# Graph attention layer: the running sum is carried through TensorE's accumulation, and ScalarE instead of VectorE writes it back and rescales it

## The chip, the core and the metric

One core of one Trainium2 chip (trn2) runs the whole program in one launch. The metric is the device time of one execution in microseconds (us). The kernel before takes 2374.6 us, the median of three executions (2372.0 to 2375.01).

## The reference

A two-layer graph network on 3125 nodes of 256 features and 53125 edges, sorted by destination. Layer 0 makes edge messages with a small MLP and an attention over heads, and sums them per node. Layer 1, in which the change lies, is a graph attention layer with four heads of 64:

```python
h = (x @ W).reshape(n, NHEAD, OUT_FEATS)
h_l = (a_l * h).sum(-1)
h_r = (a_r * h).sum(-1)
e = h_l[row] + h_r[col]
e = jnp.where(e > 0, e, ALPHA * e)
m = jax.ops.segment_max(e, row, num_segments=n)
ex = jnp.exp(e - m[row])
denom = jax.ops.segment_sum(ex, row, num_segments=n)
att = ex / (denom[row] + 1e-16)
out = jax.ops.segment_sum(att[:, :, None] * h[col], row, num_segments=n)
```

The kernel makes one pass over the edges: it keeps a running maximum, sums exp(e - running maximum) times h and the plain exponentials side by side, rescales the sum when the maximum moves, and divides at the end.

## The kernel before

Edges are sorted into 232 groups of 256 (two chunks of 128 edges), and every group belongs to one tile of 128 nodes, known only at run time from the table `gt_i`. Four groups are a batch, so there are 58 batches. Each engine runs its own instruction stream in order; the streams are tied by semaphores. In layer 1 every engine has a function `layer1(st)` that `run` calls once per step, unrolled by 16 inside a hardware loop. In step s an engine works on several groups at once, at fixed distances behind s (`st.back(d)` is the group s - d).

What the engines do in layer 1, group by group:

- GpSimd (POOL, `gather1`, L633 to L646) gathers the rows of 256 edges, by two indirect DMAs, into one of 16 slots of `row1_g`. A slot comes free when VectorE has made that slot's messages.
- TensorE (L1556 to L1609), in this order in step s: for an even step the transposition of h_r for a pair of groups (L1565, "hrT"); for group s - 3 the matmuls that spread h_r under a mask into two banks (L1579, L1582, "hr"); once a batch eight small matmuls that spread the maxima (L1594, "hm"); and for group s - 13 the sum of messages per node, two fp32 matmuls with the one-hot matrix `oneh1` as weights, into one of the two banks `agg1` (L1607, "agg").
- ScalarE (ACT, L834 to L890): once a batch index copies (L828, L829), the mask `pen` and the one-hot `onehT1` (L844, L849); once a pair the copy of hrT out of PSUM (L856); for each group two `away` and one `oneh1` activation (L860, L865) and a small copy of h_l (L875, L878, "hl"); once a batch the two exponentials `ew` and `mscale` (L886, L890).
- VectorE (DVE, L1268 to L1328): for each group the running sum of group s - 11 (L1286: tile of `acc1` plus `agg1`), the maximum (L1291), the messages of group s - 8 (L1323, "msg1"); once a batch the rescaling of the tile (L1280), the softmax steps (L1302 to L1315) and the chain of the maximum (L1240 to L1265, `top`).

A tile number is loaded from `gt_i` into registers of the engine that uses it, eight at a time, by `tiles16` (L335 to L340): before, on VectorE for L1286 and on ScalarE for the h_l copies, each twice in 16 steps.

```python
dve.tensor_tensor(acc, acc, agg1[c.slot(2)], ALU.add).then_inc(s("acc1_done"), 1)   # L1286
pe.wait_ge(s("acc1_done"), n - 1)                                                   # L1605
```

Of the kernel before, what the change touches and what calls it, by code (L numbers as in the profile page):

```python
# [30 lines left out]
P = 128  # L31
# [6 lines left out]
AHEAD = 2  # L38


class Step:
# [12 lines left out]
    def real(self):  # L54

        return not isinstance(self.k, int) or 0 <= self.n < self.total

# [32 lines left out]
def gnn_kernel(nc, x, src, dst, edge_attr_64, edge_weight, w1, b1, w2, b2, ln_w, ln_b, wq, bq, wk, bk,  # L90
# [47 lines left out]
    with ExitStack() as ctx:  # L138
# [57 lines left out]
        gt_i = sb("gt_i", [P, 16 + NG + 24], I32)  # L196
        ended = sb("ended", [P, NG])
# [10 lines left out]
        def carve(n):  # L208
# [51 lines left out]
        msg1 = carve(2 * GJ * NH1 * HE).rearrange("p (s c n) -> p s c n", s=2, c=GJ)  # L260
        hrT = carve(2 * 2 * GJ * P // 2).bitcast(BF16).rearrange("p (s n) -> p s n", s=2)
        gt_x, gt_y = (work[:, v:v + NB * ME].rearrange("p (b e) -> p b e", e=ME)
                      for v in (NT * (H + HR), NT * (H + HR) + NB * ME))
        apart = carve(NB * ME * ME).rearrange("p (b e f) -> p b e f", b=NB, e=ME)
        hq_flat = hq.rearrange("p t n -> p (t n)")
        oneh1 = hq_flat[:, 0:16 * GJ * P].rearrange("p (s c n) -> p s c n", s=16, c=GJ)
        rows_bc = work[:, 0:2 * BE].bitcast(BF16).rearrange("p (s n) -> p s n", s=4)
# [11 lines left out]
        away = sb("away", [P, 2, GJ, P])  # L279
        sc = sb("sc", [P, 2, GJ, NH0])  # L280
# [47 lines left out]
        def tiles_of(eng, k, lag, count=8):  # L328

            _, values = nc.values_load_multi_w_load_instructions(  # L330
                gt_i[0:1, bass.ds(k * 8 + (16 - lag), count)], engines=(eng,), min_val=0, max_val=NT - 1,
                skip_runtime_bounds_check_because="the table's values are bounded by the minimum with NT - 1")
            return values

        def tiles16(eng, k, lag, half):  # L335

            _, values = nc.values_load_multi_w_load_instructions(  # L337
                gt_i[0:1, bass.ds(k * 16 + (16 - lag + 8 * half), 8)], engines=(eng,), min_val=0, max_val=NT - 1,
# [22 lines left out]
        def heads_of(rows, st):  # L361

            return rows[:, st.slot(4), :].rearrange("p (h d) -> p h d", d=HE)[:, :, 0:HD1]

# [148 lines left out]
        def _(pool):  # L513
# [138 lines left out]
        def _(act):  # L652
# [167 lines left out]
            act.wait_ge(s("hr_parts"), 2)  # L820
            act_tiles = {}
# [12 lines left out]
            def layer1(st):  # L834
                g, b = st.u % BG, batch(st)
                if g == 0:
# [3 lines left out]
                    if b.real():  # L840
# [16 lines left out]
                if st.real():  # L857
                    act.wait_ge(s("srcC_ready"), b.n + 1)
                    for j in range(GJ):
                        act.activation(away[:, st.slot(2), j, :], iota1[:, :], ACT.Abs,  # L860
                                       bias=srcC[:, b.slot(4), g, j:j + 1], scale=-1.0).then_inc(s("away1"), 1)
                    act.wait_ge(s("away1"), 2 * st.n + 2)
                    if not st.first(16):
                        act.wait_ge(s("agg1_ready"), st.n - 15)
                    act.activation(oneh1[:, st.slot(16), :, :], away[:, st.slot(2), :, :], ACT.Relu, bias=1.0,  # L865
                                   scale=-1.0).then_inc(s("oneh1"), 1)
# [13 lines left out]
                e = b.back(3)  # L880
                if g == 0 and e.real():
# [6 lines left out]
                    if not e.first(2):  # L888
                        act.wait_ge(s("acc1_scaled"), e.n - 1)
                    act.activation(mscale[:, r, :], mdiff[:, r, :], ACT.Exp).then_inc(s("mscale"), 1)  # L890

            run(act, NG, 16, 9, layer1)
# [3 lines left out]
        def _(dve):  # L896
# [130 lines left out]
            def tile_table():  # L1027
# [4 lines left out]
                dve.tensor_scalar(gt_i[:, 16:16 + NG], ps[:, 6, 0:NG], float(NT - 1), None, ALU.min).then_inc(  # L1032
# [197 lines left out]
            link(dve.tensor_copy(gt_y[:, :, 0], own[:, :, 0]))  # L1230
            link(dve.tensor_tensor(apart[:, :, :, :], gt_y[:, :, :].unsqueeze(3).to_broadcast([P, NB, ME, ME]),
# [36 lines left out]
            def layer1(st):  # L1268
                g, b = st.u % BG, batch(st)
                if st.u == 0:  # L1270
                    tiles[8] = tiles16(DVE, st.k, 11, 0)
                c = st.back(11)
                if c.real():
                    acc = tile(acc1, tiles[8][st.u % 8])
                    if not c.first(1):
                        dve.wait_ge(s("acc1_done"), c.n)
                    if c.u % BG == 0:
                        k = batch(c)
                        dve.wait_ge(s("mscale"), k.n + 1)
# [4 lines left out]
                        dve.wait_ge(s("acc1_scaled"), k.n + 1)  # L1284
# [9 lines left out]
                if st.u == 7:  # L1294
# [351 lines left out]
```

## Time and profile before

| | |
|---|---|
| median of three executions | 2374.6 us |
| the profiled execution | 2369.76 us |
| its span, first to last instruction | 2368.0 us |
| busy: PE, DVE, ACT, POOL | 1942.9, 1809.6, 1484.2, 1480.6 us |

The span has an edge MLP, layer 0 and layer 1 one after the other; layer 1's loop lies at about 1597 to 2346 us. Busy times are those of the whole span and say little of one stage. A time of an instruction is its own duration; on one engine the next instruction can start a little before the last one has ended, so costs along an in-order engine are best read from start to start.

### The profile page before, as it was taken

How to read it: one execution, taken by the hardware profiler on the slowest of the kernel's cores; microseconds unless marked ns; L12 is line 12 of the kernel's file. 1: busy time of each engine (PE TensorE's matmuls, PEld its weight loads, DVE VectorE, ACT ScalarE, POOL GpSimd, SP SyncE). 2: the span in 40 equal slices, each digit the busy share in tenths (PEclk: the TensorE clock that was granted, in tenths of full speed). 3: DMA queues.
4: the chain of work that ended last, by engine and by line, in shares of the span. 5: the costliest groups of instructions: out<-in, count | busy, mean ns of one | idle time of the engine just before them, and what ended most of it. 6: DMA issues, size and time to landing. Idle time of an engine off the chain costs nothing.

```text
span 2368.0 us, 44546 instructions
## 1 busy us (share of the span) xinstructions
PE 1942.9 (82%) x9766; PEld 1418.9 (60%) x9767; DVE 1809.6 (76%) x4313; ACT 1484.2 (63%) x5321; POOL 1480.6 (63%) x1468
## 2 busy tenths in 40 slices
PE   0889999999938988889898999856777787878774
PEld 0457777777726777777776777633444454545442
DVE  7873333333339998999999999785999998999987
ACT  2236666666637777777777777447666666666660
POOL 3737777777777666666666656137666666666660
PEclk9999999999969999999999999986998988898997
DMA  8343333333339888988888885024344333333311
GB/s 239 123 183 133 131 130 132 131 130 132 122 135 328 292 298 292 299 289 300 301 290 301 303 286 169 3 69 132 102 109 107 107 103 102 107 108 101 107 36 54
DMA packets 162160, 403.34 MB, mean 170 GB/s; under 512 B 46887, under 2 KB 59099, under 8 KB 162108
## 3 DMA queue, kind: packets, MB, share of 16 engines
q0 software_dynamic: 79360, 276.09, 36.1%
q1 hardware_dynamic: 82748, 126.67, 17.0%
q8 instruction: 19, 0.31, 0.1%
q14 instruction: 33, 0.27, 0.0%
HBM read 343.89 MB, written 84.72 MB: 181 GB/s over the span
## 4 chain that ended last, share of the span: by engine, by line
PE 31%; DVE 29%; issue 16%; DMA 9%; POOL 6%; DVEq 4%; ACT 3%; SPq 0%; ACTq 0%; POOLq 0%
PE ps L1449 12%; DMA arena<-sorted_edges 6%; DVE gmx L1291 5%; POOL sorted_edges L573 4%; PE ps L1435 4%; PE ps L1482 3%; PE ps L1485 3%; DVE arena L1323 3%; DVE sc L1134 2%; PE ps L1497 2%; DVE arena L1120 2%; DVE work L1286 2%; DVEq L337 2%; PE ps L1607 2%; DVE arena L1127 2%
## 5 line engine op out<-in xcount | busy, mean ns | idle before, releaser
L642 POOL DMA_INDIRECT arena<-node_row,idxC x464 | 485.5, 1046 | 234.4 <-issue 133.1
L573 POOL DMA_INDIRECT sorted_edges<-work,idxA x416 | 404.9, 973 | 145.8 <-issue 143.1
L1091 DVE TENSOR_TENSOR work<-ps,b_bc 128x512 f32<-128x512 f32 x208 | 143.8, 691 | 322.2 <-PE ps L1449 322.2
L1449 PE MATMUL ps<-w_sb,arena 128*128 128x256 f32 x1664 | 386.7, 386 | 0.0
L1607 PE MATMUL ps<-arena,hq 128*128 128x260 f32 x928 | 281.6, 431 | 91.6 <-DVE work L1286 88.1
L1449 PEld LDWEIGHTS ps<-w_sb,arena 128*128 128x128 f32 x1664 | 307.7, 190 | 71.8 <-issue 33.8
L597 POOL DMA_INDIRECT work<-node_kvx,idxB x232 | 247.0, 1065 | 147.9 <-issue 50.9
L597 POOL DMA_INDIRECT arena<-node_kvx,idxB x232 | 246.0, 1060 | 146.1 <-issue 56.0
L712 ACT ACTIVATE work<-work 128x256 f32<-128x256 f32 x416 | 188.7, 500 | 194.1 <-DVE work L1091 194.0
L1291 DVE TENSOR_REDUCE gmx<-ps 128x4 f32<-128x1024 f32 x232 | 282.8, 1219 | 28.7 <-PE ps L1582 28.6
L1482 PE MATMUL ps<-arena,work 128*128 128x256 f32 x928 | 254.8, 398 | 57.9 <-issue 37.6
L1607 PEld LDWEIGHTS ps<-arena,hq 128*128 128x128 f32 x928 | 175.4, 210 | 133.7 <-issue 87.8
L1485 PE MATMUL ps<-arena,work 128*128 128x256 f32 x928 | 245.9, 389 | 0.0
L1497 PE MATMUL ps<-hq,work 128*128 x928 | 242.1, 384 | 1.5 <-DVE arena L1120 1.5
L1482 PEld LDWEIGHTS ps<-arena,work 128*128 128x128 f32 x928 | 161.2, 194 | 91.8 <-issue 76.6
L1579 PE MATMUL ps<-work,minus_b 128*128 128x512 bf16 x464 | 195.6, 422 | 0.7
L1485 PEld LDWEIGHTS ps<-arena,work 128*128 128x128 f32 x928 | 177.0, 196 | 31.6
L1497 PEld LDWEIGHTS ps<-hq,work 128*128 128x128 f32 x928 | 179.5, 194 | 27.2 <-issue 1.9
L1582 PE MATMUL ps<-arena,sel 128*128 128x256 bf16 x928 | 195.6, 296 | 0.0
L1134 DVE TENSOR_REDUCE sc<-arena 128x16 f32<-128x512 f32 x232 | 157.3, 678 | 22.1 <-issue 22.1
L1323 DVE TENSOR_TENSOR arena<-arena,ew 128x520 f32<-128x520 f32 x232 | 160.9, 694 | 13.0 <-PE ps L1607 11.1
L751 ACT ACTIVATE pe_<-sc,smax 128x8 f32<-128x8 f32 x464 | 135.3, 292 | 49.4 <-DVE smax L1156 48.2
(206 smaller groups left out, 3858.7 us busy)
## 6 DMA issues: line engine op xcount, KB each, us to landing
arena<-sorted_edges SPq DMA_DIRECT2D x232, 260.0 KB, 4.7
work<-sorted_rows SPq DMA_DIRECT2D x58, 256.0 KB, 3.6
arena<-in_edge_attr SPq DMA_DIRECT2D x25, 512.0 KB
node_kvx<-arena SPq DMA_DIRECT2D x24, 384.0 KB, 2.3
arena<-node_row,idxC POOLq DMA_INDIRECT x464, 3.3
sorted_edges<-work,idxA POOLq DMA_INDIRECT x416, 2.4
sorted_edges<-arena SPq DMA_DIRECT2D x25, 260.0 KB
sorted_edges<-arena SPq DMA_DIRECT2D x1, 6240.0 KB
```

The source lines that it names most:

```text
L573: pool.indirect_dma_start(rec_dram[:, :], bass.IndirectOffsetOnAxis(ap=idxA[:, st.slot(8), c:c + 1], axis=0), recA[:, st.slot(8), c, :], N ...
L597: pool.indirect_dma_start(kvx_g(st)[:, j, :], None, kvx_dram[:, :], bass.IndirectOffsetOnAxis(ap=idxB[:, st.slot(8), j:j + 1], axis=0), bo ...
L642: pool.indirect_dma_start(row1_g[:, st.slot(16), j, :], None, row1_dram[:, :], bass.IndirectOffsetOnAxis(ap=idxC[:, batch(st).slot(4), st. ...
L1134: dve.reduce_sum(sc[:, ra, :, :], heads(prod), axis=AX.X).then_inc(s("qk_sum"), 1)
L1291: dve.reduce_max(gmx[:, b.slot(2), :, 1 + g], ps[:, bank:bank + 2, :].rearrange("p c (h e) -> p (c h) e", h=2), axis=AX.X).then_inc(s("gma ...
L1323: dve.tensor_tensor(msg1[:, m.slot(2), :, :].rearrange("p c (h d) -> p c h d", d=HE), row1_g[:, m.slot(16), :, 0:HR].rearrange("p c (h d) ...
L1449: ins = pe.matmul(ps[:, 5 + t, half * H:(half + 1) * H], hidT[:, r, m, half, t * P:(t + 1) * P], w2_sb[:, m, :], start=m == 0, stop=m == 1)
L1482: pe.matmul(ps[:, 3 + r, 0:H], oneh[:, r8, j, :], msgP[:, r, j, :], start=j == 0, stop=False)
L1485: ins = pe.matmul(ps[:, 3 + r, 0:H], oneh[:, r8, j, :], msgA[:, r, j, :], start=False, stop=j == GJ - 1)
L1497: ins = pe.matmul(ps[:, 1 + r, j * H:(j + 1) * H], onehT[:, r, j, :], hq[:, bass.ds(t, 1), :].rearrange("p a n -> p (a n)"), start=True, s ...
L1579: pe.matmul(ps[:, bank + half, :].rearrange("p (h e) -> p h e", h=2), minus_b[:, :], mask.unsqueeze(1).to_broadcast([P, 2, GJ * P]), start ...
L1607: ins = pe.matmul(agg1[r], oneh1[:, r16, j, :], msg1[:, r, j, :], start=j == 0, stop=j == GJ - 1)
```

## The change

TensorE no longer sums only the group's messages: after its two matmuls it waits until the group before has been written back (`acc1_done`), and then multiplies the identity matrix with the tile of `acc1`, which is added in the same bank. The bank then holds the new running sum, and ScalarE copies it back into the tile of `acc1`, two steps later. At the last group of a batch, ScalarE's copy is made head by head with the next batch's `mscale` as a scale (a scale of 1 where the next batch begins with another tile, by the new table `same`). VectorE's addition and rescaling go away. The distances move: agg from 13 to 15 steps back, ScalarE's `oneh1` from 0 to 4, its exponentials from three batches back at a batch's first group to two back at its last. `msg1` gets eight slots in place of two, freed by the new semaphore `msg1_used`. TensorE and ScalarE load the tile numbers they now need (`pe_tiles[15]`, `act_tiles[17]`), VectorE none.

```diff
-        gt_i = sb("gt_i", [P, 16 + NG + 24], I32)
+        gt_i = sb("gt_i", [P, FRONT + NG + 24], I32)
...
             pool.memset(gmx[:, :, :, 0:1], -BIG).then_inc(s("acc1_zero"), 1)
+            pool.wait_ge(s("acc0_done"), NG)
             pool.memset(hrT[:, :, :], 0.0).then_inc(s("acc1_zero"), 1)
-            pool.wait_ge(s("acc0_done"), NG)
...
+            act.wait_ge(s("same"), 1)
...
+                if st.u % 8 == 0:
+                    act_tiles[17] = tiles16(ACT_ENGINE, st.k, 17, st.u // 8)
+                d = st.back(17)
+                if d.real():
+                    act.wait_ge(s("agg1_ready"), d.n + 1)
+                    to = acc1[:, bass.ds(act_tiles[17][st.u % 8], 1), :].rearrange("p a n -> p (a n)")
+                    if d.u % BG == BG - 1 and not d.end():
+                        k = batch(d).back(-1)
+                        act.wait_ge(s("mscale"), k.n + 1)
+                        for h in range(NH1):
+                            ins = act.activation(to[:, h * HE:(h + 1) * HE], agg1[d.slot(2)][:, h * HE:(h + 1) * HE],
+                                                 ACT.Copy, scale=mscale[:, k.slot(2), h:h + 1])
+                        ins.then_inc(s("acc1_done"), 1)
+                    else:
+                        act.copy(to, agg1[d.slot(2)]).then_inc(s("acc1_done"), 1)
...
-                    act.activation(mscale[:, r, :], mdiff[:, r, :], ACT.Exp).then_inc(s("mscale"), 1)
+                    act.activation(mscale[:, r, :], mdiff[:, r, :], ACT.Exp,
+                                   scale=same[:, bass.ds(e.n, 1)]).then_inc(s("mscale"), 1)
...
+            dve.tensor_tensor(same[:, :], gt_x[:, :, 0], gt_y[:, :, 0], ALU.is_equal).then_inc(s("same"), 1)
...
-                        dve.tensor_tensor(acc.rearrange("p (h d) -> p h d", d=HE),
-                                          acc.rearrange("p (h d) -> p h d", d=HE),
-                                          mscale[:, k.slot(2), :].unsqueeze(2).to_broadcast([P, NH1, HE]),
-                                          ALU.mult).then_inc(s("acc1_scaled"), 1)
-                    dve.wait_ge(s("agg1_ready"), c.n + 1)
-                    dve.tensor_tensor(acc, acc, agg1[c.slot(2)], ALU.add).then_inc(
-                        s("acc1_done"), 1)
...
-                    if not m.first(2):
-                        dve.wait_ge(s("agg1_ready"), m.n - 1)
+                    if not m.first(8):
+                        dve.wait_ge(s("msg1_used"), m.n - 7)
...
-                d = st.back(13)
+                if st.u % 8 == 0:
+                    pe_tiles[15] = tiles16(PE, st.k, 15, st.u // 8)
+                d = st.back(15)
...
                     for j in range(GJ):
-                        ins = pe.matmul(agg1[r], oneh1[:, r16, j, :], msg1[:, r, j, :],
-                                        start=j == 0, stop=j == GJ - 1)
-                    ins.then_inc(s("agg1_ready"), 1)
+                        ins = pe.matmul(agg1[r], oneh1[:, r16, j, :], msg1(d)[:, j, :],
+                                        start=j == 0, stop=False)
+                    ins.then_inc(s("msg1_used"), 1)
+                    if not d.first(1):
+                        pe.wait_ge(s("acc1_done"), n)
+                    pe.matmul(agg1[r], ident[:, :],
+                              acc1[:, bass.ds(pe_tiles[15][st.u % 8], 1), :].rearrange("p a n -> p (a n)"),
+                              start=False, stop=True).then_inc(s("agg1_ready"), 1)
```

The rest places the new buffers (`msg1_low`, `msg1_high`, `same`, `ended` inside `away`, a longer front of `gt_i`).

## Rows read from the trace of the kernel before

**Rows 1.** Busy time by stretch of layer 1 (length, engines' busy time, PEclk, DMA share, GB/s).

```profile
1640.90:2323.20 682.30, 537.55 (x3090) 331.70 (x3087) 619.19 (x1432) 440.34 (x1303) 452.21 (x431) 0.91 0.36 97
2323.20:2346.40 23.20, 14.37 (x53) 9.18 (x52) 17.52 (x45) 0.65 (x4) 0.00 (x0) 0.81 0.00 0
```

**Rows 2.** Groups by line, 1700 to 2300 us (count, busy, mean ns, idle before, releasers).

```profile
L642 POOL DMA_INDIRECT arena<-node_row,idxC x387 | 406.5, 1050 | 194.4 <-issue 98.9 <-DVE arena L1323 95.5
L1291 DVE TENSOR_REDUCE gmx<-ps 128x4 f32<-128x1024 f32 x194 | 236.5, 1219 | 0.7 <-PE ps L1582 0.7
L1607 PE MATMUL ps<-arena,hq 128*128 128x260 f32 x776 | 235.2, 430 | 77.0 <-DVE work L1286 73.6 <-ACT hq L865 3.0
L1286 DVE TENSOR_TENSOR work<-work,ps 128x260 f32 x193 | 81.3, 421 | 32.0 <-issue 29.3
L1594 PE MATMUL ps<-hmx,work 128*128 128x24 bf16 x384 | 17.6, 177 | 5.6 <-issue 4.1 <-DVE hmx L1260 1.2
```

**Rows 3.** Loads of eight tile numbers into registers, by line (ns min/median/max).

```profile
L337 ACTq TENSOR_LOAD <-gt_i x30: 1742/1760/1965, 1601.3 to 2313.2; - x30
...
L330 PEldq TENSOR_LOAD <-gt_i x30: 1932/1940/2520, 668.9 to 1488.5; - x30
```

**Rows 4.** Timeline of ACT in layer 1 (start, us, operation, idle before).

```profile
1919.41 0.42 ACT L865 ACTIVATE hq<-away 128x256 f32<-128x256 f32 x1
1921.46 0.20 ACT L878 COPY hmx<-hl 128x12 f32 x1 [1.64 <-issue]
...
1925.75 0.18 ACT L878 COPY hmx<-hl 128x12 f32 x1
1925.84 0.19 ACT L828 CAST idxC<-meta_s 128x8 int32 x1
...
1926.04 1.14 ACT L844 ACTIVATE work<-work,far_row 128x1024 bf16<-128x1024 bf16 x1
1927.21 1.06 ACT L849 ACTIVATE work<-work 128x1024 bf16<-128x1024 bf16 x1
1928.18 0.56 ACT L856 CAST arena<-ps 12x512 bf16<-12x512 f32 x1
1928.64 0.69 ACT L860 ACTIVATE away<-iota,srcC 128x128 f32<-128x128 f32 x2
1929.44 0.42 ACT L865 ACTIVATE hq<-away 128x256 f32<-128x256 f32 x1
1929.76 0.18 ACT L878 COPY hmx<-hl 128x12 f32 x1
...
1930.08 0.68 ACT L860 ACTIVATE away<-iota,srcC 128x128 f32<-128x128 f32 x2
```

**Rows 5.** Timeline of ACT in layer 0: a copy from PSUM, copies with a scale by partition.

```profile
1103.11 0.35 ACT L763 COPY work<-ps 128x256 f32<-128x256 f32 x1
...
1103.37 0.49 ACT L770 ACTIVATE sc<-sc,arena 128x8 f32<-128x8 f32 x2
```

**Rows 6.** Timeline of PE in layer 1, a stretch without waits.

```profile
1914.60 0.39 PE L1565 MATMUL ps<-ident_b,arena 128*12 128x128 bf16 x4
1914.92 0.39 PE L1579 MATMUL ps<-work,minus_b 128*128 128x512 bf16 x1
...
1915.80 1.04 PE L1607 MATMUL ps<-arena,hq 128*128 128x260 f32 x4
...
1916.68 0.38 PE L1579 MATMUL ps<-work,minus_b 128*128 128x512 bf16 x1
```

**Rows 7.** Timeline of PE, layer 0: the matmul behind a load of tile numbers.

```profile
1108.77 1.98 PE L1482 MATMUL ps<-arena,work 128*128 128x256 f32 x4 [1.87 <-issue]
```

**Rows 8.** Busy time by short stretch, layer 1 (columns as in rows 1).

```profile
1907.30:1909.30 2.00, 0.03 (x1) 0.06 (x1) 0.60 (x2) 1.89 (x7) 0.97 (x1) 0.58 0.44 106
1909.30:1911.30 2.00, 2.00 (x5) 1.42 (x6) 2.00 (x4) 0.26 (x1) 0.00 (x0) 0.50 0.08 32
...
1913.30:1914.60 1.30, 1.30 (x4) 0.65 (x2) 1.30 (x2) 0.00 (x0) 0.99 (x2) 0.57 0.41 106
```

More of the change, by code:

```diff
@@ L38 @@
 AHEAD = 2
+FRONT = 32
 class Step:
@@ L56, in real, with end @@
         return not isinstance(self.k, int) or 0 <= self.n < self.total
+    def end(self):
+        return isinstance(self.k, int) and self.n == self.total - 1
     def first(self, count):
@@ L259, in gnn_kernel @@
         row1_g = carve(16 * GJ * ROW1).rearrange("p (s c n) -> p s c n", s=16, c=GJ)
-        msg1 = carve(2 * GJ * NH1 * HE).rearrange("p (s c n) -> p s c n", s=2, c=GJ)
+        msg1_low = carve(4 * GJ * HR).rearrange("p (s c n) -> p s c n", s=4, c=GJ)
         hrT = carve(2 * 2 * GJ * P // 2).bitcast(BF16).rearrange("p (s n) -> p s n", s=2)
@@ L263, in gnn_kernel @@
                       for v in (NT * (H + HR), NT * (H + HR) + NB * ME))
+        at_same = NT * (H + HR) + 2 * NB * ME
+        same = work[:, at_same:at_same + NB]
         apart = carve(NB * ME * ME).rearrange("p (b e f) -> p b e f", b=NB, e=ME)
@@ L279, in gnn_kernel @@
         away = sb("away", [P, 2, GJ, P])
+        ended = away.rearrange("p r c n -> p (r c n)")[:, 0:NG]
         sc = sb("sc", [P, 2, GJ, NH0])
@@ L337, in tiles16 @@
             _, values = nc.values_load_multi_w_load_instructions(
-                gt_i[0:1, bass.ds(k * 16 + (16 - lag + 8 * half), 8)], engines=(eng,), min_val=0, max_val=NT - 1,
+                gt_i[0:1, bass.ds(k * 16 + (FRONT - lag + 8 * half), 8)], engines=(eng,), min_val=0, max_val=NT - 1,
                 skip_runtime_bounds_check_because="the table's values are bounded by the minimum with NT - 1")
@@ L363, in heads_of, with msg1 @@
             return rows[:, st.slot(4), :].rearrange("p (h d) -> p h d", d=HE)[:, :, 0:HD1]
+        def msg1(st):
+            r = st.slot(8)
+            return msg1_low[:, r, :, :] if r < 4 else msg1_high[:, r - 4, :, :]
         def kvx_g(st):
@@ L856, in layer1 @@
                     act.copy(hrT[0:PARTS, pair(c).slot(2), :], trh).then_inc(s("hrT"), 1)
-                if st.real():
-                    act.wait_ge(s("srcC_ready"), b.n + 1)
+                h = st.back(4)
+                if h.real():
+                    act.wait_ge(s("srcC_ready"), batch(h).n + 1)
                     for j in range(GJ):
[L860 to L865, printed above, removed]
+                        act.activation(away[:, h.slot(2), j, :], iota1[:, :], ACT.Abs,
+                                       bias=srcC[:, batch(h).slot(4), h.u % BG, j:j + 1], scale=-1.0).then_inc(
+                                           s("away1"), 1)
+                    act.wait_ge(s("away1"), 2 * h.n + 2)
+                    if not h.first(16):
+                        act.wait_ge(s("msg1_used"), h.n - 15)
+                    act.activation(oneh1[:, h.slot(16), :, :], away[:, h.slot(2), :, :], ACT.Relu, bias=1.0,
                                    scale=-1.0).then_inc(s("oneh1"), 1)
@@ L879, in layer1 @@
                                  own.rearrange("p a q n -> p (a q) n")).then_inc(s("hl_set"), 1)
-                e = b.back(3)
-                if g == 0 and e.real():
+                e = b.back(2)
+                if g == 3 and e.real():
                     r = e.slot(2)
@@ L887, in layer1 @@
                     act.wait_ge(s("mdiff"), e.n + 1)
-                    if not e.first(2):
-                        act.wait_ge(s("acc1_scaled"), e.n - 1)
-                    act.activation(mscale[:, r, :], mdiff[:, r, :], ACT.Exp).then_inc(s("mscale"), 1)
-            run(act, NG, 16, 9, layer1)
+                    act.activation(mscale[:, r, :], mdiff[:, r, :], ACT.Exp,
+                                   scale=same[:, bass.ds(e.n, 1)]).then_inc(s("mscale"), 1)
+            run(act, NG, 16, 17, layer1)
         @block.vector
@@ L1328, in layer1 @@
                     top(b, st)
-            run(dve, NG, 16, 11, layer1)
+            run(dve, NG, 16, 8, layer1)
             dve.wait_ge(s("acc1_done"), NG)
```

24 lines of the change are left out of this document (6 added, 18 removed).

## The prediction

> **What bounds the kernel now.** First the stretches of layer 1 [rows 1]. From TensorE's first agg matmuls at 1640.9 us (step 13) to its last hr matmuls at 2323.2 (step 234) 221 steps take 682.3 us: 3.087 us a step, 24.7 us for eight. VectorE is busy 619.19 us of it, 91%, TensorE 537.55, ScalarE 440.34, POOL 452.21. Then the groups by line, for what ends the waits [rows 2]: VectorE's maximum (L1291) waits 0.7 us in 600, so it finds its input ready, while TensorE's agg (L1607) waits 73.6 us for VectorE's addition (L1286) and POOL 95.5 us for VectorE's messages. VectorE is the bound, and the change takes work off it. The question is what is late next, since the work goes to engines that aren't idle, and into a chain.
>
> **VectorE loses** eight additions of 0.421 us in eight steps [rows 2], 3.4 us, two rescalings of the same shape, 0.8, and the idle time behind its load of tile numbers, 29.3 us over 194 groups [rows 2], 1.2. From 619.19/221 x 8 = 22.4 us busy, 18.2 remain. It stops being the bound: so much is there to win, if the others allow it. POOL's gathers with their own issue time take (406.5 + 98.9)/387 x 16 = 20.9 us for eight groups [rows 2], so POOL isn't next either.
>
> **ScalarE gains**, from start to start. A plain copy of 260 columns from PSUM stands nearest to the layer 0 copy of 256, 0.26 us to the next instruction [rows 5]; VectorE pays 0.42 for this shape [rows 2]. I take 0.30, since it also waits. The copy by heads is four activations of 65 columns with a scale by partition: two of 8 columns take 0.49 us [rows 5], two of 128 with a bias by partition 0.69 [rows 4]; between them I take 0.25 each, 1.0 in all, 1.1 to its end. A load of tile numbers lasts 1.76 us [rows 3]; the instruction behind it starts 2.05 us after the one before it, not 0.32 [rows 4]. The added load stands behind `onehT1`, which then takes 2.05 instead of 0.97.
>
> A ScalarE step, from rows 4: index copies 0.20, `pen` 1.17, `onehT1` 0.97, hrT copy 0.46, two `away` 0.80, `oneh1` 0.32, hl 0.09, exponentials 0.23. With the copies, counting from a step with loads:
> step 0: 0.20 + 1.17 + 2.05, copy 1.0, then 0.46 + 0.80 + 2.05 + 0.09 = 7.82; steps 1 and 5: 0.30 + 1.21 = 1.51; 2 and 6: 1.97; 3 and 7: 1.74; step 4: 0.20 + 1.17 + 0.97, copy 1.0, then 1.67 = 5.01. Sum 23.27 us for eight steps, already near the 24.7 of now.
>
> **TensorE gains** the identity matmul, half of agg's two: agg takes 0.88 us from start to start [rows 6], so 0.44. And it gains a load of tile numbers, which it doesn't have in layer 1 before. In layer 0 its load lasts 1.94 us [rows 3], and TensorE stands idle for 1.87 of it [rows 7]: nothing covers it. A step: hrT 0.32 (even steps), hr 0.88, agg 0.88, identity 0.44 [rows 6], hm 17.6/48 = 0.37, say 0.35, in steps 0 and 4 [rows 2]. Odd 2.20, even 2.52, step 4 2.87, step 0 with the load 4.81: 21.5 us for eight at the full clock.
>
> Each sum alone is below 24.7. **But the change ties the two engines**. ScalarE's copy in step t takes what TensorE's identity matmul made in step t - 2; the identity matmul of step s waits for ScalarE's copy in step s + 1. There is no second tile in flight: one engine can be ahead by a step at most. So ScalarE's long steps (0 and 4, where the copy comes behind the index copies, `pen`, `onehT1` and the load) hold TensorE, and TensorE's long step (0) holds ScalarE, and what follows the wait on TensorE, hrT, hr and hm, VectorE's and ScalarE's input, is queued behind it.
>
> I follow the chain once round, with 0.65 us from an identity matmul's start to the copy (half of the 1.04 of four [rows 6], 0.52, and 0.13 that I choose for the drain and the signal), and 0.45 back (0.35 [rows 5] and a chosen 0.10). The starts, ScalarE's step 0 at zero:
> copy(0) 3.42; identity(7 of before) at 3.42 + 1.15 = 4.57. TensorE's step 0 follows: 4.57 + 0.44 + 0.32 + 0.88 + 0.35 + 1.94 + 0.88 puts identity(0) at 9.38. ScalarE is ready for copy(2) at 9.33 and gets it at 10.03. Identity(1) 11.58; copy(3) 12.23; identity(2) 14.10; copy(4) 16.31; TensorE is ready at 16.30 but identity(3) waits for that copy until 17.46. Copy(5) 18.98; identity(4) 20.33; copy(6) 20.98; identity(5) 22.53; copy(7) 23.18, and ScalarE's next step 0 starts at 24.92. So 24.92 us at the full clock, of which ScalarE waits 1.65; nothing is left of VectorE's saving.
>
> **The clock.** When TensorE stood idle for 2.0 us at 1907.3, its granted clock went to 0.50, 1.2 GHz, and stayed there to about 1914.0, some 5 us of work [rows 8]. In layer 0, too, four matmuls behind the load took 1.98 us [rows 7], where a stretch without a wait takes 1.04 [rows 6]. After the change a wait of 2.2 us (identity(7): ready at 27.25, released at 29.49) and the load's 1.9 follow each other within five us, in every eight steps. So I take agg, identity and the next hr behind the load at half the clock: 0.88 + 0.44 + 0.88 = 2.20 us more, all in the chain: 27.12 us for eight steps. That VectorE's load no longer stops TensorE is in this, as the waits of now are in the 24.7.
>
> **The sum.** Steps 15 to 234 are 219 steps, 27.4 times eight, each 27.12 - 24.70 = 2.42 us longer: 66 us. Made against the profiled 2369.76 that is 2436; the median shown lies 4.8 above it, so 2374.6 + 66 = 2440.6, say 2440.
>
> What I cost at nothing: the tail. Now 23.2 us pass from the last hr matmuls to the last addition [rows 1]; after, 12 groups' sums of 0.88 + 0.44, one load of 1.94 and the last copy make 19 us at the full clock, more at the half (the row's clock is 0.81): between -4 and +13, taken as 0. The wait for `same` is one VectorE operation, at most an addition's 0.42 us [rows 2], once. The moved hrT memset has the whole projection ahead of its first reader, the wider tables are only addresses; eight `msg1` slots take away a wait of VectorE, which is off the path.
>
> **A rule to weigh.** The idle row [rows 7] says that the load on TensorE isn't covered. The Trainium skill, "TensorE: Matmul & The Clock Gate", section "Step-by-step: what each phase is for", says that TensorE's sequencer takes the next instruction as soon as one is committed and does not wait for the drain. By that, work queued ahead would cover a load; by the row it costs its 1.9 us. The row decides, because in the chain too TensorE has just waited and has little queued.
>
> **The rivals.** First, the other side, faster: the load on TensorE is covered by queued matmuls. Then identity(0) comes at 8.27, and the chain closes after 23.99 us, bound by ScalarE: -0.71 x 27.4 = -19 us, 2355 (23.27, -39 us, if no wait at all were left). For it speaks that each engine's own sum is below 24.7; against it the 1.87 us of idle [rows 7]. It decides from the point where the load and what follows cost TensorE under 1.5 us. Chance 0.17. The rule above leads there.
> Second, the clock holds: the chain as above, 24.92 us, +6 us, 2381, and up to 25.9 (+33 us) with small waits at hrT and gathers that I left out. For it speaks that TensorE gets more work, and that the clock is 0.91 over the loop [rows 1] with stretches at the full one; against it rows 8. Chance 0.28.
> Third, the clock falls at the wait already, before the load: hrT, hr and hm of step 0 cost 1.55 us more, 28.67, +109 us, 2484. Chance 0.15, in the forecast's own range.
> The forecast, 26 to 28.2 us for eight steps, has 0.40.
>
> **The numbers.** About 0.2%, 4.7 us, is what a measurement of this kernel can tell from no change. Faster by more: 0.17, the first rival. Within: 0.08, the lower end of the second. Slower: 0.20 of the second, 0.15 of the third and the forecast's 0.40 make 0.75. The range runs from 2365, inside the first rival, to 2488, just over the third.
>
> **What would show it.** Right: in the loop VectorE's maximum waits for TensorE instead of being ready; TensorE idles about 1.9 us by "issue" at each load, twice in 16 steps, with the clock at 0.50 behind it; the identity matmul waits for ScalarE's copy at steps 3 and 7, longest behind ScalarE's load; ScalarE's copy waits for TensorE behind TensorE's load. Eight steps take 26 to 28 us. Wrong: eight steps below 24.7 us with ScalarE busy nearly throughout, or a TensorE without idle time at its loads; or POOL's gathers back to back with nothing waited for, which would make 20.9 us the bound.

## The result and the profile after

The changed kernel takes 2396.28 us (median of eight executions, 2391.45 to 2402.62), the kernel before, run beside it, 2375.41 (2372.0 to 2387.89): a ratio of 1.0074, 95% interval 1.0058 to 1.0089. It is 20.9 us slower. The direction is the forecast one, the size a third of the 66 us forecast.

The profiled execution took 2395.59 us with a span of 2393.8. Its stretches, in the columns of [rows 1] (the busy time and count of PE, PEld, DVE, ACT, POOL, then PEclk, DMA share and GB/s): from the first agg matmuls (now step 15) to the last hr matmuls, the tail behind them, and 600 us out of the middle.

```profile
1652.80:2346.60 693.80, 589.74 (x3502) 403.62 (x3500) 520.87 (x1152) 541.29 (x1684) 439.69 (x429) 0.95 0.36 95
2346.60:2372.20 25.60, 20.59 (x89) 15.03 (x87) 10.07 (x27) 8.12 (x29) 0.00 (x0) 0.93 0.00 0
1700.00:2300.00 600.00, 506.60 (x2991) 346.02 (x2990) 443.95 (x981) 465.48 (x1446) 385.59 (x375) 0.94 0.38 101
```

VectorE fell from 91% busy to 75% (520.87 of 693.80), as meant. But 219 steps in 693.8 us are 25.34 us for eight, where [rows 1] gave 24.70: 27.4 x 0.64 = 17.6 us. The tail went from 23.2 to 25.6, another 2.4. That is 20.0 of the 20.9 us. The two profiled executions lie further apart than that, 25.8 us, because the loop also starts later in the one after. POOL's first gather of layer 1 in the timeline of after (start, us, engine, line, operation, idle before):

```profile
1605.89 1.04 POOL L654 DMA_INDIRECT arena<-node_row,idxC  x1 [10.94 <-issue]
```

The same row in the timeline of before:

```profile
1597.54 1.04 POOL L642 DMA_INDIRECT arena<-node_row,idxC  x1 [10.50 <-issue]
```

In ten further runs of the changed kernel's variants that gather starts anywhere between 1602.6 and 1611.6 us, always later than in the one profile of before, which is itself 5 us faster than its median. I put nothing of the loop down to it; whether a few microseconds of it belong to the change can't be told from a single profile of before.

Who waits for whom, 1700 to 2300 us, after (engine, what, line, releaser: us in total, times, longest):

```profile
DVE gmx L1304 <- PE ps L1593: 136.9, 93, 4.3
...
POOL arena L654 <- DVE hq L1334: 99.6, 45, 5.0
...
PE ps L1625 <- ACT work L875: 72.8, 47, 2.4
ACT work L879 <- PE ps L1625: 60.9, 87, 2.1
...
PE ps L1620 <- ACT work L879: 13.7, 11, 1.5
```

VectorE's maximum waited 0.7 us before [rows 2] and waits 136.9 now: VectorE is no longer the bound. In its place stand the two waits of the new circle: TensorE's identity matmul (L1625) for ScalarE's copy by heads (L875), 47 times 1.5 us, and ScalarE's plain copy (L879) for the identity matmul, 87 times 0.7. POOL, which waited for VectorE before, still does, and VectorE now waits for TensorE itself.

The groups that the change made, by line, 1700 to 2300 us, in the columns of [rows 2]:

```profile
L1625 PE MATMUL ps<-work,ident 128*128 x373 | 121.3, 408 | 72.8 <-ACT work L875 72.8
L879 ACT COPY work<-ps 128x260 f32 x140 | 52.5, 375 | 61.6 <-PE ps L1625 60.9
L875 ACT ACTIVATE work<-ps,mscale 128x65 f32 x188 | 43.5, 314 | 25.1 <-issue 25.1
```

The loads of tile numbers after, in the columns of [rows 3]; TensorE now has 30 of them in layer 1:

```profile
L345 ACTq TENSOR_LOAD <-gt_i x60: 1736/1754/1943, 1607.9 to 2369.9; - x60
...
L345 PEldq TENSOR_LOAD <-gt_i x30: 1932/1935/1948, 1634.0 to 2357.4; - x30
```

**One turn of eight steps.** I measure turns on ScalarE from the `pen` (L857) of a step with TensorE's load to the second `pen` after it. Between 1700 and 2300 us there are 23 such turns after: 15 take 24.4 to 25.3 us (mean 24.82) and eight 27.0 to 27.3 (mean 27.15). The mean of all is 25.63; before it was 24.84. By the granted clock, 1.2 GHz in a fall and 2.4 otherwise, each of the eight long turns has a long fall (6 to 7 us at half the clock); five of the 15 short ones have a short fall (3 to 4 us; mean turn 25.00), and ten have none (mean turn 24.73). TensorE's timeline shows the difference: its rows of 1906 to 1911 us are from a short turn, which ScalarE's index copy starts at 1902.03, the others from a long one:

```profile
1906.76 0.70 PE L1625 MATMUL ps<-work,ident 128*128 x2 [2.34 <-ACT work L875]
...
1908.37 0.38 PE L1593 MATMUL ps<-arena,sel 128*128 128x256 bf16 x2
1908.59 0.35 PE L1605 MATMUL ps<-hmx,work 128*128 128x24 bf16 x8
1910.46 1.14 PE L1620 MATMUL ps<-arena,hq 128*128 128x260 f32 x4 [1.52 <-ACT work L879]
1911.44 0.60 PE L1625 MATMUL ps<-work,ident 128*128 x2
...
2006.20 0.70 PE L1625 MATMUL ps<-work,ident 128*128 x2 [2.34 <-ACT work L875]
...
2008.18 0.63 PE L1593 MATMUL ps<-arena,sel 128*128 128x256 bf16 x2
2008.61 0.41 PE L1605 MATMUL ps<-hmx,work 128*128 128x24 bf16 x8
2009.89 2.10 PE L1620 MATMUL ps<-arena,hq 128*128 128x260 f32 x4 [0.86 <-ACT work L879]
2011.78 1.07 PE L1625 MATMUL ps<-work,ident 128*128 x2
```

The same wait of 2.34 us opens both (in every other turn it is about 2.05). In the first, agg takes 1.14 us behind the load; in the second, four matmuls take 2.10 us, and the hr matmuls ahead of the load are slow already (0.63 for 0.38). The granted clock of the second (stretches of 2 us, columns as above) is at half, 1.2 GHz, from within 2006 to 2008 to about 2014:

```profile
2004.00:2006.00 2.00, 0.00 (x0) 0.00 (x0) 1.97 (x5) 0.94 (x6) 1.45 (x2) 1.00 0.86 195
2006.00:2008.00 2.00, 1.80 (x10) 1.02 (x11) 0.18 (x1) 1.50 (x5) 1.64 (x2) 0.86 0.59 154
2008.00:2010.00 2.00, 1.14 (x12) 0.73 (x10) 1.15 (x2) 0.85 (x4) 1.36 (x2) 0.50 0.36 102
...
2012.00:2014.00 2.00, 2.00 (x7) 0.95 (x7) 0.00 (x0) 1.01 (x3) 1.56 (x2) 0.50 0.26 69
```

In the short turn every stretch from 1904 to 1916 has 1.00. One thing to read with care: the profile puts the idle time ahead of agg down to ScalarE's copy L879. Agg needs the copy of two groups back (L875, step 0), not that one. What ended last is TensorE's load, which has a row of its own (kind, how many, ns, start):

```profile
L345 PEldq TENSOR_LOAD <-gt_i x1: 1932/1932/1932, 1908.1 to 1908.1; - x1
```

It starts at 1908.1, while the hr matmuls are still running, and ends 0.4 us ahead of agg. So 0.8 us of it run beneath hr and hm, and 1.52 us of idle time are left; in the turns with the wait of 2.05 us the load starts 0.5 us sooner behind the identity matmul, and 0.9 us are left. Such a turn at the full clock:

```profile
1827.95 0.70 PE L1625 MATMUL ps<-work,ident 128*128 x2 [2.05 <-ACT work L875]
...
1831.02 1.11 PE L1620 MATMUL ps<-arena,hq 128*128 128x260 f32 x4 [0.89 <-issue]
```

A turn with a short fall, between 1932 and 1936 us, has the same wait, and its load leaves no idle time, since hr and hm run beneath it at half the clock:

```profile
1931.68 0.70 PE L1625 MATMUL ps<-work,ident 128*128 x2 [2.06 <-ACT work L875]
...
1934.79 1.58 PE L1620 MATMUL ps<-arena,hq 128*128 128x260 f32 x4
```

### The profile page after: what moved, and what is told of

Same layout as the page of the kernel before. It is cut to its first block, busy times and chain, and to the rows that moved or that the text cites. A ratio compares the mean times of both kernels' runs of the same rounds, so it can differ in the third digit from the quotient of the medians.

```text
span 2393.8 us, 45972 instructions
## 1 busy us (share of the span) xinstructions
PE 2014.1 (84%) x10230; PEld 1505.0 (63%) x10231; DVE 1707.3 (71%) x4024; ACT 1592.5 (67%) x5724; POOL 1475.1 (62%) x1468
## 4 chain that ended last, share of the span: by engine, by line
PE 48%; DVE 14%; issue 11%; ACT 11%; DMA 7%; ACTq 4%; POOL 3%; DVEq 1%; SPq 0%; POOLq 0%
PE ps L1460 16%; DMA arena<-sorted_edges 6%; PE ps L1446 5%; PE ps L1620 5%; PE ps L1493 4%; PE ps L1496 4%; PE ps L1625 3%; PE ps L1508 3%; ACTq L345 3%; ACT work L857 2%; PE ps L1590 2%; PE ps L1593 2%; DVE arena L1150 2%; DVE sc L1164 2%; ACT work L875 2%
## 5 line engine op out<-in xcount | busy, mean ns | idle before, releaser
L654 POOL DMA_INDIRECT arena<-node_row,idxC x464 | 475.9, 1026 | 261.0 <-issue 141.1
L1625 PE MATMUL ps<-work,ident 128*128 x464 | 150.4, 407 | 81.7 <-ACT work L875 81.5
L1590 PE MATMUL ps<-work,minus_b 128*128 128x512 bf16 x464 | 190.1, 410 | 1.1 <-DVE gmx L1304 1.1
L1164 DVE TENSOR_REDUCE sc<-arena 128x16 f32<-128x512 f32 x232 | 157.2, 678 | 22.8 <-issue 22.6
L890 ACT ACTIVATE away<-iota,srcC 128x128 f32<-128x128 f32 x464 | 160.1, 393 | 0.0
L1625 PEld LDWEIGHTS ps<-work,ident 128*128 128x128 f32 x464 | 85.8, 196 | 117.1 <-issue 106.0
```

The costliest lines, as they stand in the source:

```text
L654: pool.indirect_dma_start(row1_g[:, st.slot(16), j, :], None, row1_dram[:, :], bass.IndirectOffsetOnAxis(ap=idxC[:, batch(st).slot(4), st. ...
L1164: dve.reduce_sum(sc[:, ra, :, :], heads(prod), axis=AX.X).then_inc(s("qk_sum"), 1)
L1590: pe.matmul(ps[:, bank + half, :].rearrange("p (h e) -> p h e", h=2), minus_b[:, :], mask.unsqueeze(1).to_broadcast([P, 2, GJ * P]), start ...
L1625: pe.matmul(agg1[r], ident[:, :], acc1[:, bass.ds(pe_tiles[15][st.u % 8], 1), :].rearrange("p a n -> p (a n)"), start=False, stop=True).th ...
```

## The experiments

The theory after the result: the circle between ScalarE's copy and TensorE's identity matmul, with TensorE's load and ScalarE's two loads in it, bounds the loop, and the clock adds some 2.3 us in a part of the turns only. Rivals: VectorE still sets the pace; the circle costs nothing and the falls of the clock are the whole loss; the copies by head are it. Each row below is against the kernel before on the same chip; turns (those that begin with TensorE's load) and clock are those of 1700 to 2300 us; before has a mean turn of 24.84 and a clock of 0.91. The last column has the turns in which the granted clock stays at 2.4 GHz. e10 turned out to be the kernel after once more, so its 24.47 beside 24.73 says how well such a mean is known.

| run | median, us | ratio to before, interval | turn: mean (range), us | clock | without a fall: mean, us (turns) |
|---|---|---|---|---|---|
| after | 2396.28 | 1.0074 [1.0058, 1.0089] | 25.63 (24.4 to 27.3) | 0.94 | 24.73 (10 of 23) |
| e8_dve_more | 2399.19 | 1.0088 [1.0062, 1.0113] | 25.44 (24.3 to 27.3) | 0.94 | 24.70 (8 of 24) |
| e1_tile0 | 2355.73 | 0.9893 [0.9857, 0.9928] | 23.97 (23.5 to 24.6) | 0.99 | 23.90 (21 of 23) |
| e2_load_after | 2367.67 | 0.9929 [0.9899, 0.9959] | 24.37 (23.7 to 25.0) | 0.98 | 24.17 (18 of 24) |
| e3_copy_earlier | 2354.93 | 0.9880 [0.9843, 0.9918] | 24.02 (23.1 to 26.3) | 0.99 | 23.88 (22 of 24) |
| e7_one_copy | 2351.49 | 0.9883 [0.9845, 0.9921] | 23.93 (23.0 to 26.5) | 0.98 | 23.52 (20 of 24) |
| e4_busy | 2385.52 | 1.0012 [0.9994, 1.0030] | 24.95 (24.6 to 25.1) | 1.00 | 24.95 (24 of 24) |
| e10_two_loads | 2391.22 | 1.0056 [1.0035, 1.0076] | 25.38 (24.1 to 27.3) | 0.94 | 24.47 (9 of 24) |
| e11_two_loads | 2495.08 | 1.0492 [1.0464, 1.0521] | 29.07 (28.2 to 30.0) | 0.88 | none of 21 |
| e5_both | 2342.17 | 0.9848 [0.9819, 0.9878] | 23.42 (22.6 to 24.0) | 0.99 | 23.34 (21 of 24) |
| e6_covered | 2355.15 | 0.9898 [0.9855, 0.9941] | 24.34 (22.9 to 26.3) | 0.96 | 23.71 (12 of 23) |

**Is VectorE still the bound?** Behind every maximum VectorE makes a spare addition of 208 columns.

```diff
+                    dve.tensor_tensor(scratch[:, :], ar_bc[:, 0:208], al_bc[:, 0:208], ALU.add).then_inc(
+                        s("spare"), 1)
```

> The changed kernel with a spare VectorE addition of 208 columns (about 0.37 us) behind every maximum, about what was taken off VectorE. If VectorE is off the path as the profile says (it waits 137 us in 600 for TensorE), the time stays within 10 us of 2396; what the addition does is to delay the messages and the maxima by 0.4 us. If VectorE still bounds or shares the chain, 0.37 x 232 = 86 us at most.

The busy time of the 600 us, and VectorE's wait in it:

```profile
1700.00:2300.00 600.00, 510.10 (x3011) 347.33 (x3010) 497.38 (x1176) 470.44 (x1459) 397.81 (x378) 0.94 0.37 102
```
```profile
DVE gmx L1305 <- PE ps L1599: 84.8, 61, 3.4
```

VectorE does 53 us more (497.38 for 443.95), takes it out of its wait (84.8 for 136.9), and the turn is no longer. VectorE is off the path: this rival falls.

**Is TensorE's load in the circle?** First without the load: the identity matmul always reads tile 0.

```diff
-                if st.u % 8 == 0:
-                    pe_tiles[15] = tiles16(PE, st.k, 15, st.u // 8)
...
-                              acc1[:, bass.ds(pe_tiles[15][st.u % 8], 1), :].rearrange("p a n -> p (a n)"),
+                              acc1[:, 0:1, :].rearrange("p a n -> p (a n)"),
```

> The changed kernel without TensorE's load of tile numbers: the identity matmul always reads tile 0 of the sum (so the running sums of the other tiles are left out). The chain theory (TensorE and ScalarE hold each other, the uncovered load is part of the chain): eight steps at the full clock take 24.0 us in place of 25.0, 27.4 times 0.9 = 25 us off 2396, some 2371; and where TensorE's idle stretch at the load is gone the clock should fall seldom, which takes up to 20 us more off. The rival that ScalarE alone is the bound: no change, 2390 to 2400, since ScalarE's instructions are the same. The rival that only the clock matters: the turns of 27 us vanish and those of 25.0 us stay, some 2373, so the length of the turns at the full clock tells it from the chain.

Then with the load moved behind the agg matmuls that don't need it:

```diff
-                if st.u % 8 == 0:
-                    pe_tiles[15] = tiles16(PE, st.k, 15, st.u // 8)
                 d = st.back(15)
...
                     ins.then_inc(s("msg1_used"), 1)
+                if st.u % 8 == 0:
+                    pe_tiles[15] = tiles16(PE, st.k, 15, st.u // 8)
+                if d.real():
```

> The changed kernel with TensorE's load moved behind the two message matmuls, which then run while it loads: 0.9 us of the load's 1.9 is covered. Chain theory: eight steps at the full clock 24.0 to 24.2 us in place of 25.0, 22 to 27 us off 2396, some 2370 to 2375, and the clock falls less often. ScalarE alone the bound: no change. Only the clock: less than 10 us off, with the turns at the full clock still 25.0 us.

Without the load a turn takes 23.97 us, where the prediction's chain with a covered load had 23.99. By the ratios this run is 43 us under the changed kernel, as expected with most of the falls gone, and the one with the load moved is 34 us under it, somewhat more than the expected 22 to 27. With the load behind agg, TensorE's timeline shows agg queued ahead of it:

```profile
1904.01 0.35 PE L1605 MATMUL ps<-hmx,work 128*128 128x24 bf16 x8
1904.22 1.12 PE L1618 MATMUL ps<-arena,hq 128*128 128x260 f32 x4
1906.09 0.70 PE L1626 MATMUL ps<-work,ident 128*128 x2 [0.75 <-ACT work L879]
```

From agg to the identity matmul 1.87 us pass, as from hm to agg in the kernel after, and 1.12 of them are now work; the idle time is 0.75 in place of 1.52. Half of the load's idle time was its place in the order.

**Is ScalarE's copy, behind `onehT1`, what TensorE waits for?** `onehT1` is moved behind the copy; then, in another kernel, the four copies by head are one plain copy.

```diff
-                        act.wait_ge(s("pen"), b.n + 1)
-                        if not b.first(4):
-                            act.wait_ge(s("hm_mm"), b.n - 3)
-                        act.activation(onehT1[:, b.slot(4), :], pen[:, b.slot(2), :], ACT.Relu, bias=1.0,
...
+                if g == 0 and b.real():
+                    act.wait_ge(s("pen"), b.n + 1)
+                    if not b.first(4):
+                        act.wait_ge(s("hm_mm"), b.n - 3)
+                    act.activation(onehT1[:, b.slot(4), :], pen[:, b.slot(2), :], ACT.Relu, bias=1.0,
...
                 c = st.back(2)
```

> The changed kernel with ScalarE's copy of the sum ahead of onehT1 (behind pen) in a batch's first step, so that TensorE gets the sum 1.0 to 1.2 us earlier there. ScalarE's own work stays the same within 0.2 us. Chain theory: TensorE's waits of 2.3 and 0.9 us at these steps shrink by about 1.1 and 0.9; eight steps at the full clock 24.0 to 24.5 us in place of 25.0, 14 to 27 us off 2396. ScalarE alone the bound: at most 5 us off. Only the clock: as its idle stretches change, with the turns at the full clock still 25.0 us.

```diff
-                    if d.u % BG == BG - 1 and not d.end():
+                    if False:
```

> The changed kernel with one plain copy in place of the four by head at a batch's last group (the rescaling is left out). It takes 0.7 us off ScalarE at the two steps where TensorE waits for it. Chain theory: about 1.2 us for eight steps, turns of 23.7 to 24.0 us at the full clock, 33 us off 2396 and some more with fewer falls of the clock: 2350 to 2365. If the load on TensorE is the only thing that matters: no change, 2390 to 2400.

Each takes 1.6 to 1.7 us out of a turn. A part of that is the clock's, since with TensorE's longest wait for ScalarE's copy down from 2.4 us to 1.1 (e3) and 1.8 (e7) most falls are gone. The rest is the circle's, and the turns without a fall show it: 0.6 to 0.9 us less in e3, 0.9 to 1.2 in e7. The copy of steps 0 and 4 is there earlier by `onehT1`'s 0.97 us in the one kernel, and done sooner by 0.94 - 0.38 = 0.6 us, twice in a turn, in the other. Both runs are some 45 us under the changed kernel by the ratios; for e3 that is more than the 14 to 27 expected. The copies by head are a part of it, not the whole: one copy in their place leaves a turn at 23.93, as moving them does.

**What do the clock's falls cost?** Spare matmuls of 248 columns into unused columns of the bank keep TensorE at work: four ahead of the identity matmul of each eighth step, three ahead of the load. The three, and so the load behind them, first wait until ScalarE has copied the bank out, for which agg waits in the kernel after.

```diff
+                    pe.wait_ge(s("acc1_done"), st.back(15).n - 1)
+                    for j in range(3):
+                        pe.matmul(ps[:, 5 + 2 * st.back(15).slot(2), 260:508], ident[:, :], W_sb[:, 0, 0:248],
+                                  start=True, stop=True)
...
+                    if st.u % 8 == 7:
+                        for j in range(4):
+                            pe.matmul(ps[:, 5 + 2 * r, 260:508], ident[:, :], W_sb[:, 0, 0:248],
+                                      start=False, stop=False)
```

> The changed kernel with TensorE kept busy where it waits most: four spare fp32 matmuls of 248 columns ahead of the identity matmul in every eighth step (1.7 us, where it waits 2.3) and three ahead of its load, into columns of the banks that nobody reads. They add no work that anyone waits for. If the clock's fall comes from these waits, the granted clock in the loop goes to 0.98 or more and the turns of 27.1 us vanish: 9 of 23 turns by 2.1 us, over 27.4 turns 23 us off 2396, some 2373. If the fall costs nothing, or doesn't come from the waits, 2396 stays, or it becomes up to 20 us slower if the three matmuls delay the load.

The stretch of 600 us, and TensorE around the load:

```profile
1700.00:2300.00 600.00, 563.85 (x3415) 400.27 (x3414) 457.14 (x1010) 478.80 (x1493) 391.30 (x385) 1.00 0.39 101
```
```profile
1902.29 1.84 PE L1630 MATMUL ps<-W_sb,ident 128*128 128x248 f32 x8
1904.79 0.70 PE L1634 MATMUL ps<-work,ident 128*128 x2 [0.67 <-ACT work L875]
...
1906.62 0.35 PE L1605 MATMUL ps<-hmx,work 128*128 128x24 bf16 x8
1906.83 1.50 PE L1612 MATMUL ps<-W_sb,ident 128*128 128x248 f32 x6
1908.48 1.11 PE L1625 MATMUL ps<-arena,hq 128*128 128x260 f32 x4 [0.15 <-ACT work L879]
```

The clock holds throughout, no turn is above 25.1 us, and the mean is 24.95: the prediction's chain at the full clock had 24.92. The time is that of before (1.0012), which is the second rival's +6 us (here 2385.52 - 2379.77 = 5.75). By the ratios, 1.0074 against 1.0012, the falls cost the changed kernel 15 us; 23 were expected. That is rather too little, since the spare matmuls don't seem to be quite free: the turns are 0.2 us longer than those of the kernel after without a fall (0.5 longer than those of e10). By these turns the falls cost 25.63 - 24.73 = 0.90 us a turn, 25 us in all. The 1.50 us of spare work also shows what runs under the load: from hm to agg 1.86 us pass here, 1.87 in the kernel after.

**Does the idle time settle how often the clock falls?** A second load of tile numbers on TensorE. The first try asked for the same entries twice:

```diff
+                    pe_tiles[0] = tiles16(PE, st.k, 15, st.u // 8)
```

> Question: what decides how often TensorE's clock falls behind its load. The load of eight tile numbers on TensorE is issued twice in a row; all else is as after the change. Both theories: the second load adds up to its 1.94 us to the chain, so a turn of eight steps at the full clock takes 24.9 + 1.9 = 26.8 us (24.4 to 25.3 becomes 26.3 to 27.2). Theory A (the idle time settles it: the two waits of 2.3 and 1.5 us in the kernel after are near the point at which the clock falls, and a longer idle time makes it fall nearly always, as the prediction had assumed for one load): turns of 28.5 to 29.3 us nearly throughout, mean near 28.9, which is 27.4 x (28.9 - 25.6) = 90 us more than the kernel after, about 2485 us; granted clock between 1700 and 2300 us about 0.90. Theory B (whether it falls is settled by something else than the idle time): falls in about 4 turns of 10 as in the kernel after, mean 27.5 us, 53 us more, about 2450 us, clock 0.94. A third outcome, turns still near 25.6 us, would say that the second load overlaps the first.

The trace has 30 loads, as after: the second one wasn't made, and the run is a repeat of the kernel after (six of 24 turns above 26 us). Then with the second load one entry further on, and used in odd steps:

```diff
+                    pe_tiles[16] = tiles_at(PE, st.k, 16 - 8 * (st.u // 8) - 2)
...
-                              acc1[:, bass.ds(pe_tiles[15][st.u % 8], 1), :].rearrange("p a n -> p (a n)"),
+                              acc1[:, bass.ds(pe_tiles[15 + st.u % 2][st.u % 8 - st.u % 2], 1), :].rearrange("p a n -> p (a n)"),
```

> Question: what decides how often TensorE's clock falls behind its load. In the run before this one the second load was the first one over again and the trace has one load a turn, 30 in the loop, as after the change. Now the second load begins one entry further in the table: even steps of a turn take their tile number from the first load, odd steps from the second, and nothing else differs from the kernel after. Both theories: the second load adds up to 1.94 us to the chain, so a turn of eight steps at the full clock takes 26.3 to 27.2 us. Theory A (the length of TensorE's idle time settles it: the waits in the kernel after are near the point at which the clock falls, and longer ones make it fall nearly always, as the prediction had assumed for one load): turns of 28.5 to 29.3 us nearly throughout, mean near 28.9, 27.4 x (28.9 - 25.6) = 90 us more than the kernel after, about 2485 us; granted clock between 1700 and 2300 us about 0.90. Theory B (something else than the idle time settles it): falls in about 4 turns of 10 as in the kernel after, mean 27.5 us, 53 us more, about 2450 us, clock 0.94. A third outcome, turns still near 25.6 us, would say that the second load overlaps the first.

TensorE around the loads, in one turn:

```profile
2031.88 0.70 PE L1633 MATMUL ps<-work,ident 128*128 x2 [2.05 <-ACT work L882]
...
2033.71 0.35 PE L1612 MATMUL ps<-hmx,work 128*128 128x24 bf16 x8
2037.07 1.83 PE L1628 MATMUL ps<-arena,hq 128*128 128x260 f32 x4 [3.01 <-ACT hq L903]
2038.70 1.07 PE L1633 MATMUL ps<-work,ident 128*128 x2
```

Theory A holds: the clock falls in each of the 21 turns, agg behind the loads takes 1.4 to 2.1 us (1.14 where the clock holds), the mean turn is 29.07 us and the time 2495. The prediction's own chain with one more load, 24.92 + 1.94, and 2.20 for the clock make 29.06, but so close a match is luck: the turns are of two kinds, some 28.3 us with a short fall, and some 29.8 with a longer one.

**The best order.** The moves of e2 and e3 together:

> The changed kernel with TensorE's load behind the message matmuls and ScalarE's copy ahead of onehT1, both together. Chain theory, followed round once more: with both long waits short, ScalarE's own 23.1 us for eight steps is what is left; against e3_copy_earlier (turns of about 23.9 us, 2355 us) 0.75 us a turn, 20 us less: some 2335. If the two edits remove the same wait (each alone is enough), the time stays near e3_copy_earlier, 2350 to 2357.

2342.17 us: 36 us under the kernel before beside it (2378.06), and the fastest of all. By the ratios it is 8 us under e3, where 20 were expected, and the two intervals overlap; that the moves add up rests on the turn, 23.42 us against 24.02. The waits of the circle, to be held against those of after:

```profile
DVE gmx L1305 <- PE ps L1594: 91.4, 90, 2.2
...
PE ps L1577 <- ACT arena L886: 31.2, 50, 0.7
ACT work L874 <- PE ps L1627: 26.3, 72, 1.0
...
PE ps L1627 <- ACT work L870: 21.1, 26, 1.1
```

TensorE's wait for the copy by heads fell from 72.8 to 21.1 us, ScalarE's for the identity matmul from 60.9 to 26.3. TensorE's wait for the hrT copy (L886) is new, 31.2 us: `onehT1`, moved behind the copy of the sum, stands directly ahead of it. One more step, ScalarE's second load (that of the hl copies) moved up behind `onehT1`:

```diff
+                if st.u % 8 == 0:
+                    act_tiles[2] = tiles16(ACT_ENGINE, st.k, 2, st.u // 8)
                 c = st.back(2)
                 if c.u % 2 == 0 and c.real():
```

> As e5_both, and ScalarE's second load (for the h_l copies) directly behind onehT1, whose 1.06 us then run beside it: ScalarE's eight steps fall from 23.1 to 22.4 us. If ScalarE is what bounds e5_both: 0.65 x 27.4 = 18 us below it, some 2317. If TensorE (21.5 us of work and its waits) or POOL (20.9) has become the bound: less than 6 us below it.

By the medians it is 13 us slower than e5, where up to 18 us faster were expected. The load now stands ahead of the hrT copy, on which TensorE's next hr matmuls wait:

```profile
ACT work L874 <- PE ps L1627: 69.5, 92, 3.0
...
PE ps L1577 <- ACT arena L888: 48.7, 50, 1.4
```

TensorE's wait for the hrT copy (L888) grew from 31.2 us in e5 to 48.7, the clock fell to 0.96, and ScalarE's wait for the identity matmul is back. By these waits the idle time on ScalarE wasn't on the path where it stood, and is where it was put; no run tests that apart from the clock, which falls in 11 of 23 turns here and in three of 24 in e5.

## Why the prediction came out as it did

- **VectorE stops being the bound: right.** 18.2 us of work in a turn were forecast; 443.95 us in 600 at 25.63 a turn are 19.0. e8 shows that 53 us more of it cost nothing.
- **The chain: right in its sum.** In the short turn, from the index copies at 1902.03: ScalarE's copy of step 0 at 3.64 us (3.42 forecast), identity(7) at 4.73 (4.57), identity(0) behind the load at 9.41 (9.38), ScalarE's copies of steps 2 and 4 at 10.15 and 16.39 (10.03, 16.31), the next step 0 at 25.10 (24.92). The turns without a fall take 24.73 on average, and e4, where the clock holds, 24.95. Sizes in it are off and cancel nearly: hm and load were charged 0.35 + 1.94, and take 1.87 from hm's start to agg's, since the load starts while hr and hm are still queued; the wait of 2.2 us that precedes is 2.34, and each of ScalarE's copies is a little later. (From a copy by heads to the identity matmul the prediction adds 1.15 us, where its own 1.1 and 0.10 make 1.20.)
- **The clock: the failed step.** That a wait of 2.2 us and the load's 1.9 "follow each other within five us, in every eight steps" is what happened; that agg, identity and the next hr then run at half the clock in each of them is not. Of 23 turns eight were long, five had a short fall that cost some 0.3 us, and ten had none. So the term of 2.20 us a turn measured 0.90 (25.63 - 24.73), while the chain came out 0.1 below before (24.73 against 24.84), where 0.22 above was forecast. Over the whole loop 27.4 x 2.42 = 66 us became 27.4 x 0.64 = 17.6. The size of a long turn came out right, 27.15 us on average against 27.12, but with luck: in the long turn shown the clock falls ahead of the load already, and for longer than agg, identity and hr, but a part of that lies under the load. I took one stretch of the trace before, [rows 8], in which an idle time of 2.0 us was followed by half the clock, and one load, [rows 7], as if such a time always did that. In the kernel after, both lengths of the first wait, 2.05 and 2.34 us, are followed by the full clock and by half of it. With longer idle time (e11) the clock falls in every turn; with only one of the two waits shortened it falls in fewer: in six of 24 turns in e2, all short (the second wait at most 0.78 us), and in two of 24 in e3, one of them long (the first wait at most 1.1). The changed kernel lies between. The length of the waits alone doesn't tell in which of two turns the clock falls; what does, no run here was made to show, and it stays open.
- **What the trace of before held.** Its clock was no better: 0.91, where the changed kernel has 0.94, so the 24.70 that the forecast is held against had falls in it already. And it could have told that a fall is no certainty: of 26 loads on TensorE in layer 0 with 1.86 to 1.94 us of idle time behind them, half the clock followed eight, [rows 7] among them. The load ahead of that one has the same idle time, and the same four matmuls take 1.13 us in place of 1.98:

```profile
1082.32 1.13 PE L1482 MATMUL ps<-arena,work 128*128 128x256 f32 x4 [1.87 <-issue]
```

- **The rivals.** The second, the clock holding, is true of ten turns in 23, and nearly of five more, and gave a time 15 us too low; the forecast is true of one in three. The third, a fall at the wait already, is what the long turn at 2006 shows (hr slow ahead of the load), but the load's own idle time then shrinks from 1.52 to 0.86 us, since the load isn't slowed, and the turn grows by 2.4 us and not by 3.75. The first, the load covered, is true in part: 0.8 to 1.3 of the load's 1.93 us run beneath queued matmuls in the changed kernel at the full clock, and more in e2.
- **The rule on queued work.** The row was held to decide, with little queued and 1.9 us idle. That is half right: hr and hm were queued, and 1.5 or 0.9 us stayed idle, by turns. Where agg is queued ahead of the load (e2), or spare matmuls (e4), they run beneath it. The Trainium skill, "TensorE: Matmul & The Clock Gate", section "Step-by-step: what each phase is for", says that the sequencer goes on to the next instruction once one is committed; the load that starts under hr, e2 and e4 agree. The same page, section "HAM oscillation — how this bites in real kernels", has it that a wait in every pass of a loop can start each pass at the low clock, and that reordering the loop so that TensorE's work stays together cures it; e11 agrees with the first and the kernel after in part (13 of 23 turns); e2, which puts agg directly behind hm, agrees with the second but for its short falls (0.98 from 0.94).
- **The tail: right.** Between -4 and +13 us, taken as 0; it measured +2.4.

## What to carry to other kernels

When work is moved off the bounding engine, sum the others, but then follow the new dependency once round: here every engine had room, and the circle of one copy and one matmul took it all. In such a circle the order of instructions is worth more than their number: two moves that remove no instruction (what isn't needed for the copy behind it; a register load behind matmuls already queued) made 2342 us out of 2396. Whether the clock falls behind idle times of some 2 us was a matter of how often here, so price it with a share, and take the share from all such idle times in the trace before, not from one: eight of 26 there, eight long falls in 23 turns after.

## What the runs showed that I had not expected

- With the same waits (2.05 or 2.34 us, then the load) ten turns kept TensorE's clock, five lost it for 3 to 4 us and eight for 6 to 7.
- A long fall costs a turn 2.4 us and a short one 0.3: a part of either lies under the load, which takes 1.93 to 1.95 us at both clocks.
- A copy of 260 columns from PSUM takes ScalarE 375 ns, and four of 65 columns with a scale 0.94 us from the first start to the last end (L875, x4); VectorE's addition of the same 260 columns took 421 [rows 2].
